# Magnitudes of the side rows in 16 bits, and their maximum with a constant as two operations

## What is computed

```python
xb = x.reshape(sh[:-1] + (sh[-1] // BLOCK, BLOCK))
amax = jnp.max(jnp.abs(xb), axis=-1, keepdims=True)
sc = jnp.clip(amax / FP4_MAX * global_scale, 0.0, FP8_MAX)
sc8 = sc.astype(jnp.float8_e4m3fn).astype(jnp.float32)
dq = sc8 / global_scale
...
a = jnp.clip(jnp.abs(xb) / safe_dq, 0.0, FP4_MAX)
q = jnp.sign(xb) * _FP4_VALS[jnp.digitize(a, _FP4_MIDS)]
...
x = x + jnp.tanh(g_xattn[3]) * _L3_xattn_ref(_layernorm(x, axis=-1), ctx_1024, ...)
x = x + jnp.tanh(g_ffn[3]) * _L3_ffn_ref(_layernorm(x, axis=-1), ...)
```

## Time and profile before

| | |
|---|---|
| time, median of 3 runs | 1058.82 us (1058.22 to 1059.3) |
| the profiled execution's own time | 1061.08 us |
| its span, first to last instruction | 1059.3 us |
| busy: PE, PEld, DVE, ACT, POOL | 896.4, 694.4, 873.2, 679.0, 577.7 us |
| mean granted clock of PE | 0.899 |
| last attention with side groups | about 822 to 915 us of the span |
| last feed-forward | about 915 us to the end |

### The profile page before, as it was taken

The page is one execution under the profiler, slowest core; times in us unless marked ns, Lnnn a source line. Parts: engine busy times, 40 slices in busy tenths (PEclk is TensorE's granted clock), DMA queues, the critical chain, the costliest instruction groups (busy, mean ns, idle before and its releaser), DMA issues.

```text
span 1059.3 us, 30026 instructions
## 1 busy us (share of the span) xinstructions
PE 896.4 (85%) x11481; PEld 694.4 (66%) x11481; DVE 873.2 (82%) x2299; ACT 679.0 (64%) x1740; POOL 577.7 (55%) x691
## 2 busy tenths in 40 slices
PE   8999999999999963699959999988889999634553
PEld 5888879988887751366638888844458778412232
DVE  5999988878899974256649999869978999799997
ACT  5888864367777730245438888868867788544553
POOL 6444402243457667322178888235553788667644
PEclk9999999999999976799989999969999999755555
DMA  8760000000000011465311111000000000000000
GB/s 223 177 256 3 2 2 2 2 2 3 3 17 27 28 37 52 123 186 150 103 43 35 32 33 33 7 1 1 2 2 3 2 2 3 1 5 16 15 21 25
DMA packets 60527, 44.43 MB, mean 42 GB/s; under 512 B 15196, under 2 KB 55781, under 8 KB 59366
## 3 DMA queue, kind: packets, MB, share of 16 engines
q1 hardware_dynamic: 55718, 34.09, 11.0%
q0 software_dynamic: 4096, 8.34, 2.7%
q10 hardware_dynamic: 576, 0.13, 0.1%
HBM read 23.73 MB, written 18.87 MB: 40 GB/s over the span
## 4 chain that ended last, share of the span: by engine, by line
PE 53%; DVE 19%; POOL 12%; issue 9%; ACT 3%; DMA 2%; DVEq 1%; POOLq 0%; SPq 0%; ACTq 0%
PE ps L777 8%; PE ps L735 8%; PE ps L708 6%; PE ps L618 4%; POOL big L1248 3%; PE ps L749 3%; PE ps L821 3%; PE ps L812 3%; PE ps L813 3%; PE ps L528 3%; DVE rowmax L1976 2%; POOL slots L1264 2%; PE ps L672 2%; PE ps L628 2%; DVE big L1848 2%
## 5 line engine op out<-in xcount | busy, mean ns | idle before, releaser
L1976 DVE TENSOR_REDUCE rowmax<-ps 128x16 f32<-128x1024 f32 x128 | 155.4, 1214 | 25.8 <-PE ps L708 24.8
L1982 DVE TENSOR_TENSOR sm<-ps,rowmax 128x512 f32<-128x512 f32 x256 | 164.9, 686 | 3.4
L1084 ACT ACTIVATE pr<-ps 128x512 f32<-128x512 f32 x256 | 139.0, 595 | 43.7 <-PE ps L777 39.2
L777 PE MATMUL ps<-cst,sm 128*128 128x128 f32 x1024 | 140.2, 277 | 11.6 <-DVE sm L1982 9.2
L735 PE MATMUL ps<-vbd,pr 128*64 128x18 f32 x4096 | 141.6, 212 | 0.6 <-ACT pr L1084 0.5
L735 PEld LDWEIGHTS ps<-vbd,pr 128*64 128x64 f32 x4096 | 133.9, 138 | 5.2 <-ACT pr L1084 1.6
L777 PEld LDWEIGHTS ps<-cst,sm 128*128 128x128 f32 x1024 | 112.4, 141 | 27.0 <-issue 18.5
L1407 POOL TENSOR_SCALAR xn<-x_sb,mv_all,rstd_all 128x128 f32<-128x128 f32 x122 | 97.5, 799 | 35.7 <-PE ps L672 28.5
L963 ACT ACTIVATE qbd<-ps,bqp,cst 128x128 f32<-128x128 f32 x256 | 104.9, 465 | 5.7 <-PE ps L688 1.9
L1248 POOL DMA_INDIRECT big<-expert_out,row_g x64 | 68.6, 1072 | 38.6 <-DMA expert_out<-xn_all 23.0
L1264 POOL DMA_INDIRECT slots<-xn_all,row_s x64 | 65.0, 1015 | 34.4 <-DVE sm L1982 18.2
(11 more groups left out here) (314 smaller groups left out, 2356.2 us busy)
## 6 DMA issues: line engine op xcount, KB each, us to landing
slots<-hT SPq DMA_DIRECT2D x8, 1024.0 KB, 11.9
sm<-slots SPq DMA_DIRECT2D x32, 256.0 KB, 3.1
expert_out<-xn_all SPq DMA_DIRECT2D x16, 256.0 KB, 3.0
ew<-in_L_ffn_w SPq DMA_DIRECT2D x24, 128.0 KB, 2.6
out<-x_sb SPq DMA_DIRECT2D x32, 64.0 KB, 1.5
slots<-xn_all,row_s POOLq DMA_INDIRECT x64
big<-expert_out,row_g POOLq DMA_INDIRECT x64, 2.7
x_sb<-in_x SPq DMA_DIRECT2D x1, 512.0 KB, 4.5
```

The lines of the kernel that those rows point to most:

```text
L777: last = nc.tensor.transpose(turned[b][:, r * P:(r + 1) * P], sm[x][:, c:c + P], ident)
L1084: nc.scalar.activation(pr[y][:, b, :], turned[b], ACT.Exp, scale=SCALE).then_inc(p_ready[y], 1)
L1976: v.tensor_reduce(row3, sc, AX.X, ALU.max).then_inc(rowmax_ready[x], 1)
L1982: v.tensor_tensor(sm[x][:, :].rearrange("p (r g k) -> p r g k", r=RG, k=S)[:, part], sc[:, part], row3[:, part].unsqueeze(3).broadcast_to( ...
```

## The change

The magnitudes `side_m` become 16-bit numbers in the first half of the same place; so ACT writes 16 bits (L1005), POOL's maximum reads and writes 16 bits (L1341), and the sum and the difference (L1342, L1345) read one 16-bit and one 32-bit operand. The maximum with the constant is given as two operations of one instruction, the same maximum twice, where before the second was left empty. The instructions of every engine, their order and their waits stay as they were.

```diff
-        side_m = zero[:, 2 * SIDE * D:3 * SIDE * D]
+        side_m = zero[:, 2 * SIDE * D:2 * SIDE * D + SIDE * D // 2].bitcast(BF16)
...
-                side_step(m, 7, nc.gpsimd.tensor_scalar(side_m, side_m, 1.5 * 2.0 ** 22, None, ALU.max))
+                side_step(m, 7, nc.gpsimd.tensor_scalar(side_m, side_m, 1.5 * 2.0 ** 22, 1.5 * 2.0 ** 22, ALU.max, ALU.max))
                 side_step(m, 8, nc.gpsimd.tensor_tensor(rows, side_m, rows, ALU.add))
```

## The result

The changed kernel takes 1061.06 us (median of 18 runs, 1059.85 to 1062.69), the kernel before 1058.97 us in runs beside it (18 runs, 1057.81 to 1061.27). The ratio is 1.0018 with a 95% interval of 1.0012 to 1.0025: about 2 us slower, told from no change only by the number of runs. I had said 1059.7, that is +0.9.

A forecast was written before the change was run, and what follows sets the result against it. PE and DVE were taken to bound the attention with next to no slack, DVE the feed-forward. Feed-forward -1.2, L1962 +1.3, L1800 +0.9 and -0.07 gave +0.9 us: 1059.7, range 1057.0 to 1061.7.

The forecast's parts named there:

- Step 7 at 0.61: POOL's maximum L1341 would fall from 1.50 to 0.61 us, like L1346, 0.89 shorter, eight times.
- My upper bound of 3.2: Longest time allowed for POOL's L1341, up to 3.2 us, from the rate of L1407, a two-operation instruction of 32-bit rows.
- Steps 8 and 9 at nothing: POOL's sum and difference (L1342, L1345), now reading a 16-bit operand, would not change; ends 0.2 us each either way.
- What bounds the two stages: Last attention: PE and a DVE loop of equal length, next to no slack; last feed-forward: DVE, taking turns with POOL.
- L1962 as the price: Last attention: DVE's tiny L1962 would wait for POOL's earlier L1345, +0.33 us in each of four rounds, +1.3.
- my 2.2 with L1800 and less 0.07: Attention terms: L1962 +1.3 us, L1800 held by L1428 +0.9 (0.23 a round), fifth round's present loss of 0.07 gone.
- The feed-forward in turns: Last feed-forward, two groups: POOL and DVE alternate, so only 0.61 of 0.89 us is won in each; sum -1.2.
- The sum: Whole kernel: -1.2 + 1.3 + 0.9 - 0.07 = +0.9 us, median from 1058.82 to 1059.7.
- rounds of 16.5: Sign in the last attention: rounds would take 16.5 us instead of 15.98.
- a longer L1800: Sign in the last attention: DVE's L1800 at 0.35 us or more, against 0.21 before.
- an earlier L1852: Sign in the last feed-forward: L1852 would come about 0.6 us sooner after L1341's start.
- My rival on the slower side: L1341 shrinks only partly, say to 1.2 us, and L1962 loses 0.92 a round: +3.3, 1062.1 us; chance 0.13.

The follow-up runs named there:

- 16 bits alone: The kernel before with magnitudes `side_m` in 16 bits and step 7 (L1341) still one maximum; ratio 1.0045 (1.0029 to 1.006) to the kernel before.
- 32 bits, minimum and maximum: The kernel before with `side_m` in 32 bits as before and L1341 as minimum with 2**100, then maximum with the constant; ratio 0.9993 (0.9985 to 1.0002).
- the pair alone: The kernel before with `side_m` in 32 bits as before and L1341 taking the same maximum twice; ratio 1.0007 (0.9996 to 1.0018).

## Why the prediction was right, and where it was not

- **Step 7 at 0.61: wrong, and in direction.** This is the term that failed: 0.89 saved eight times was 0.43 lost eight times. I took the row of the nearest shape, step 10, and let both of its properties, 16 bits and two operations, stand for its speed. It has a third, the kind of the two operations, and among the forms tried that alone decides. My upper bound of 3.2 held the value, and the row behind it, a two-operation instruction of another kind, was nearer to the truth than the one that I took. The rule that I quoted from the Trainium skill (GPSIMD Engine Reference, section 3.1) is contradicted by the runs: 1.49 us for one operation where it would give, as an estimate, 0.44 plus dispatch, while minimum and maximum, dispatch and all, take 0.61.
- **Steps 8 and 9 at nothing: off by 0.11 each**, inside the stated 0.2. I had compared multiplications with a broadcast operand, which do not show it. In the experiment with 16 bits alone this 0.1 decides 4 us.
- **What bounds the two stages: right.** PE and DVE share one loop in the attention, and a delay in front of L1976 goes through whole. Taking L1962 away from both kernels made their attentions equal.
- **L1962 as the price: right, but held by another operation.** I had L1345 in front of it for +0.33 in four rounds; it was L1428 for +0.31 in four, and L1345 for +0.22 in the fifth only (L1962 901.62 to 902.08, L1345 ending at 902.06). The attention lost 1.44 in all, against my 2.2 with L1800 and less 0.07. The Trainium skill (SBUF — State Buffer, "Who interferes with whom") says that the one that comes second waits for the whole instruction of the other; the cases given here (two in the earlier trace rows, two in the changed kernel, one each with 16 bits only and with 32 bits, minimum and maximum), with L1962 ending 0.02 to 0.03 us behind the end of POOL's operation in each, agree. L1800 itself took 0.16 in the changed kernel; where POOL did run early it was held as I had worked out.
- **The feed-forward in turns: right for the case that I had**, -1.21 against -1.2 where L1341 takes 0.61. In the changed kernel, with a later POOL, it is +0.42.
- **The sum: near for the wrong reason.** +0.9 was the right side, but two errors stand in it: -1.2 for the feed-forward should have been +0.4, and +2.1 for the attention should have been +1.4. That the result lies 1 us from the forecast is luck: I expected a loss from a POOL that comes 0.9 earlier, and got one from a POOL that comes 0.3 later. Where POOL did come earlier as I had it, the same sum missed: -0.7 us (-1.6 to 0.2) instead of +0.9, and +0.2 by the distances, because the attention lost 1.4 instead of 2.1. Of the signs that I had named, L1341 at 0.61, L1342 near 1275 ns, rounds of 16.5, a longer L1800 and an earlier L1852 all failed; L1962 near 0.50 and a late L777 came. My rival on the slower side (the saving too small, L1962 longer) was nearest, but I worked it out only for savings, never for a POOL that comes later.

## What to carry to other kernels

Measure an operation in its very form before costing it: a row of the same shape and width but of another kind of operation is no bound. When an operation off the critical path changes its length, by even 0.1 us, ask what each one behind it will newly coincide with on an engine whose instructions it has been seen to hold. A short one of the critical engine, of 0.17 us, can be held for the whole of a long one, 1.2 us here. To find out, take away the one that is held, together with a control that takes it from the kernel before.

## What was not expected of the hardware

- On POOL, 128x512 elements in SBUF: an instruction with constants takes 1.49 us with one operation (maximum, minimum or sum), 1.92 with two (maximum twice, maximum and minimum, product and maximum), and 0.61 where the two are minimum and then maximum. 16 or 32 bits makes no difference to a maximum and to the pairs of minimum and maximum.
- Sums and differences of two tensors do depend on width: 1.26, 1.16 and 1.04 us with none, one and two 16-bit operands (the last a tile with itself).
- A DVE operation of four columns took 1.16 us when a POOL operation of two tensors had started 0.03 us before it, and still its usual 0.17 us when it came 0.13 us before the end of one (L1407, 851.88 to 852.68, with L1962 at 852.55, in the kernel with the pair alone).
